# A graph layer on one Trainium2 core: edge ranges found to the edge, 17 gathers per 128 nodes, a ring of four

## The chip, the cores and the metric

One of the eight cores of a Trainium2 chip runs the kernel. The metric is the device time of one launch in microseconds (us). The engines are TensorE (PE, with its weight loads as PEld), VectorE (DVE), ScalarE (ACT), GpSimd (POOL) and SyncE (SP). They run their own instruction streams and wait for each other through semaphores.

## The reference

One layer over 12500 nodes with 256 channels and 200000 edges, sorted by destination. Everything is float32.

```python
xn = layernorm(x)
# relational graph convolution, 8 relations: mean over (relation, destination)
msg = xn[src] * edge_weight[:, None]
seg = edge_type * N + dst
h = segment_sum(msg, seg) / maximum(segment_sum(1, seg), 1)
gnn = einsum('rnc,rco->no', h.reshape(R, N, C), weight) + xn @ root + bias
# linear attention, 8 heads of 32, over all nodes: q, k = elu(.) + 1
mix = (q @ (k^T v)) / (q . sum(k) + 1e-6) @ wo + bo
x = x + gnn + mix
# mixture of 6 experts with 3 layers of 256 x 256, the best two of a router's softmax
x = x + ffn(layernorm(x))
```

Because the relation's weight acts on a sum, the kernel computes y[node, relation] = xn[node] @ weight[relation] for all nodes first. An edge then adds coefficient x y[src, type] to its destination, where the coefficient is its weight over the number of edges of the same destination and type.

## The kernel before, in words

The program has two phases, a block each. A matmul in float32 precision is made of three fast ones: each operand is split into a high part (ACT, a rounding copy) and a low part (DVE, the difference).

**First phase** (lines 85 to 762). A loop over 98 steps `u` of 128 nodes. PE computes keys and values (line 696, `pproj`) and the eight relations' products (`yb`), ACT copies the latter to `yst` (line 314, two buffers), SP stores them to the table `y_tab` in memory (line 242). Every fourth step a super-tile of 512 nodes is loaded, normalised, turned and stored as `xt_tab`. The function `edges(u)`, which DVE (line 531) and PE (line 714) have each, hangs work on the edges on single steps: the edge arrays are loaded twice, as 391 rows of 512 edges (`rows_i`) and as 125 rows of 1600 edges (`lin_d`, `lin_t`, `lin_w`, line 215). From the first, PE's transposes (`turn_rows`, line 707) and DVE's copies (`by_tile`, line 408) make tables that stay in SBUF with one column for each tile of 128 edges: destination `dst_t`, row of `y_tab` `idx_t`, coefficient `coef_t`. From the smallest and largest destination of each tile, `tiles_of_nodes` (line 419) finds for each 128 nodes the first tile of edges (`lo_row`) and by how many tiles it exceeds 18 (`more_row`). From the second, scans in both directions count the edges of the same destination and type; the coefficient goes to memory at step 80 as `coef_tab` (line 231), comes back at step 82 as rows (`crow`, line 235), and is turned at steps 86 to 90.

**Second phase** (from line 764). 25 super-tiles of 4 x 128 nodes; the last has two times 128. For each 128 nodes the edges are gathered tile by tile, 18 tiles from `lo` on; edges of other nodes in them match no column of the one-hot tile. A super-tile n thus has 72 gathers, in 12 portions p of 6:

- POOL: `portion(n, p)` (line 1045) waits until portion p - 3 has been used, then issues six indirect DMAs (line 1025), each of which gathers 128 rows of 1 KB from `y_tab` into the ring `ring`, which has three slots. `indices(n)` (line 1039) copies the row numbers from `idx_t` to `ring_i`. After the last super-tile two portions of a 26th, empty one are gathered.
- ACT: `high(n, p)` (line 1080) waits for the rows and writes coefficient x row to `row_hi` (two buffers, line 1088).
- DVE: `one_hot(n, p)` (line 1220) compares destinations with 0 to 127 into `sel` (two buffers), `low_rows(n, p)` (line 1225) writes the difference to `row_lo`. `tables(n)` (line 1209) copies destinations and coefficients of a super-tile.
- PE: `aggregate(n, p)` (line 1502) does two matmuls a tile, `sel` times high and low rows, into `acc`, and counts `portion_used`, which frees the slot.
- `leftover` (in each of the four) would handle, one by one, tiles beyond the 18.

The loop `iteration(i, plan)` (25 times, on PE, ACT and DVE) finishes super-tile i (layer norm, router, six experts) and in between aggregates super-tile i + 1 and computes its queries and attention. The order is written out by hand: portions 0 and 1 after the turned features, 2 after the first hidden layer, 3, 4, 5, 7, 9, 11 in front of the third layer of experts 0 to 5 (`AHEAD_W3`) and 6, 8, 10 behind that of experts 2, 3, 4 (`BESIDE_W3`). ACT does portions 6, 8 and 10 in halves between hidden features (line 1102 high part, 1104 full value), and, at the end of iteration i, portions 0 and 1 of super-tile i + 2, ahead of the root of the variance (line 1107) of the next iteration. PE's experts are line 1453, root sums and queries too.

**Between the phases**: SP loads the weights (`stage`, two buffers), ACT and DVE split three expert weights (lines 1158 and 1416) before they take any portion of super-tile 0; then all 12 portions of it follow without experts. `portions_before(n, p)` (line 944) turns a portion into a count.

## Time and profile before

| what | value |
|---|---|
| median of three runs | 3529.99 us (3527.38 to 3536.67) |
| the profiled execution | 3521.7 us, span 3519.7 us |
| mean granted clock of TensorE | 0.94 |
| first phase, from the start to the last store's wait | 0 to about 815 us |
| stage between the phases, to the first root of variance | 815 to 964 us |
| 24 loop iterations | 964 to 3477 us |
| last iteration | 3477 to 3520 us |

The page names a group of instructions by line, engine, operation and tiles (output <- inputs). PE, DVE, ACT and POOL are busy while they compute; POOL's `DMA_INDIRECT` is the time it takes to write a gather's descriptors. "Idle before" is the time the engine stood still ahead of an instruction, with what ended it; "issue" means that the profile shows nothing that it waited for.

### The profile page before, as it was taken

The page shows a single profiled execution, that of the slowest core. Times are in us where ns is not written, and L with a number is a line of the kernel's source. Part 1 is how long each engine was busy: PE and PEld are TensorE (multiplying, and loading weights), DVE is VectorE, ACT ScalarE, POOL GpSimd, SP SyncE. Part 2 cuts the span into 40 slices and gives each one's busy share as a digit, 9 for nine tenths or more (in the row PEclk, how much of TensorE's full clock was granted, in tenths as well). Part 3 has the DMA queues.
Part 4 walks back from the last instruction along what each step waited for, and adds up shares of the span by engine and source line. Part 5 has one row for each costly group of instructions (what it writes and reads, how often), then busy time and mean ns, then how long its engine had stood idle before and what let it go on. Part 6 is the DMA issues. An engine that isn't in the chain of part 4 may idle for free.

```text
span 3519.7 us, 49971 instructions
## 1 busy us (share of the span) xinstructions
PE 3073.8 (87%) x17125; PEld 2680.3 (76%) x17126; DVE 2454.4 (70%) x5692; ACT 2104.1 (60%) x4161; POOL 1975.6 (56%) x1932
## 2 busy tenths in 40 slices
PE   5999999994488988889988888888888898888887
PEld 4888888884377877878877777777787787777776
DVE  3458745323477777877777777778787777787775
ACT  4555555553366666666666666666666666666665
POOL 0000000003777777777777777777777777777773
PEclk9999999996599999999999999999999999999999
DMA  5445455545333333333343333333333333333331
GB/s 198 171 170 194 189 193 199 203 172 177 94 110 113 113 115 108 112 100 116 114 117 109 113 101 116 113 116 116 111 114 101 113 113 115 109 117 98 112 98 53
DMA packets 159285, 450.16 MB, mean 128 GB/s; under 512 B 33711, under 2 KB 79953, under 8 KB 140122
## 3 DMA queue, kind: packets, MB, share of 16 engines
q0 software_dynamic: 86976, 237.62, 23.9%
q1 hardware_dynamic: 68220, 205.82, 15.7%
q10 hardware_dynamic: 3826, 3.43, 0.3%
q8 instruction: 138, 2.26, 0.3%
q14 instruction: 125, 1.02, 0.1%
HBM read 303.73 MB, written 143.01 MB: 127 GB/s over the span
## 4 chain that ended last, share of the span: by engine, by line
POOL 35%; PE 19%; issue 17%; DVE 2%; ACT 2%; POOLq 1%; DVEq 0%; DMA 0%; ACTq 0%
POOL ring L1025 35%; PE bank L1453 13%; PE acc L1508 4%; DVE row_lo L1229 2%; ACT row_hi L1088 2%; PE bank L1598 1%; POOLq L1041 1%; PE bank L1480 1%; PE bank L1580 0%; DVE h_lo L1327 0%; POOLq L1042 0%; POOLq L951 0%; ACT ht L1104 0%; PE acc L1525 0%; PE acc L1453 0%
## 5 line engine op out<-in xcount | busy, mean ns | idle before, releaser
L1025 POOL DMA_INDIRECT ring<-y_tab,ring_i x1812 | 1945.3, 1074 | 682.7 <-issue 530.6
L1088 ACT ACTIVATE row_hi<-ring,coef_w 128x256 fp32r<-128x256 f32 x1812 | 764.0, 501 | 457.4 <-issue 397.4
L1229 DVE SCALAR_TENSOR_TENSOR row_lo<-ring,coef_w,row_hi 128x256 fp32r<-128x256 f32 x1806 | 740.5, 477 | 160.3 <-ACT row_hi L1088 160.3
L1508 PE MATMUL acc<-row_hi,sel 128*128 128x256 f32 x1800 | 521.6, 319 | 323.1 <-DVE row_lo L1229 323.1
L1102 ACT ACTIVATE h_hi<-bank,bias_t 128x512 fp32r<-128x512 f32 (+1 forms) x600 | 405.8, 676 | 445.6 <-PE bank L1453 433.8
L1508 PEld LDWEIGHTS acc<-row_hi,sel 128*128 128x128 f32 x1800 | 388.7, 216 | 357.1 <-DVE row_lo L1229 352.3
L1327 DVE TENSOR_TENSOR h_lo<-ht,h_hi 128x512 fp32r<-128x512 f32 (+1 forms) x600 | 401.8, 679 | 338.9 <-ACT ht L1104 336.7
L696 PE MATMUL yb<-wr_hi,xhl 128*128 128x512 f32 x1568 | 509.1, 395 | 0.0
L1508 PE MATMUL acc<-row_lo,sel 128*128 128x256 f32 x1800 | 505.3, 310 | 0.0
L1042 POOL COPY ring_i<-idx_t 128x18 int32 x104 | 26.2, 289 | 812.0 <-POOLq L88 810.6
L1104 ACT ACTIVATE ht<-bank,bias_t 128x512 f32<-128x512 f32 (+1 forms) x600 | 405.9, 676 | 27.9 <-DVE h_lo L1327 25.7
L314 ACT ACTIVATE yst<-yb 128x512 f32<-128x512 f32 x392 | 230.8, 595 | 320.0 <-PE yb L696 314.0
L1508 PEld LDWEIGHTS acc<-row_lo,sel 128*128 128x128 f32 x1800 | 393.0, 218 | 4.8
L1453 PE MATMUL bank<-ew_hi,h_hi 128*128 128x256 f32 x1176 | 351.7, 299 | 19.5 <-DVE h_lo L1327 18.8
L696 PEld LDWEIGHTS yb<-wr_hi,xhl 128*128 128x128 f32 x1568 | 294.6, 188 | 72.3
L1453 PE MATMUL bank<-ew_lo,h_hi 128*128 128x256 f32 x1176 | 339.7, 289 | 0.0
L1453 PE MATMUL bank<-ew_hi,h_lo 128*128 128x256 f32 x1176 | 338.7, 288 | 0.0
L696 PE MATMUL yb<-wr_lo,xhl 128*128 128x512 f32 x784 | 310.1, 396 | 0.0
L1222 DVE TENSOR_TENSOR sel<-iota_w,rel_w 128x768 fp32r<-128x768 f32 x301 | 286.2, 951 | 6.3 <-issue 6.3
L659 DVE TENSOR_TENSOR zk<-pproj,bkv_sb 128x256 f32<-128x256 f32 x98 | 41.6, 424 | 347.1 <-PE pproj L696 346.1
L1453 PE MATMUL bank<-h_hi,ew_hi 128*128 128x512 f32 (+1 forms) x600 | 260.4, 434 | 3.0 <-DVE h_lo L1327 3.0
L1453 PEld LDWEIGHTS bank<-ew_hi,h_hi 128*128 128x128 f32 x1176 | 232.1, 197 | 30.3 <-DVE h_lo L1327 28.1
(240 smaller groups left out, 5647.2 us busy)
## 6 DMA issues: line engine op xcount, KB each, us to landing
y_tab<-yst SPq DMA_DIRECT2D x97, 1024.0 KB, 3.8
ring<-y_tab,ring_i POOLq DMA_INDIRECT x1812, 2.8
xt_tab<-xhl SPq DMA_DIRECT2D x25, 1024.0 KB, 3.8
xc<-xt_tab SPq DMA_DIRECT2D x25, 1024.0 KB, 4.9
xs<-in_x SPq DMA_DIRECT2D x24, 512.0 KB, 5.9
x<-in_x SPq DMA_DIRECT2D x48, 256.0 KB
out<-y SPq DMA_DIRECT2D x24, 512.0 KB
stage<-in_L_ffn_expert_w SPq DMA_DIRECT2D x6, 768.0 KB, 11.5
```

Of the source, the lines that this page charges most:

```text
L314: act.activation(yst[:, h, 2 * b:2 * b + 2, :], yb[(YB * u + b) % 3][:, :].rearrange("p (r n) -> p r n", r=2), ACT.Copy).then_inc(y_ev, 1)
L659: dve.tensor_tensor(zk[:, h, :], pproj[:, 0:C], bkv_sb[:, 0:C], ALU.add)
L696: last = pe.matmul(out_ap, a, b, start=(i == 0), stop=(i == len(parts) - 1))
L1025: pool.indirect_dma_start(out=out_ap, out_offset=None, in_=y_tab[:, :], in_offset=bass.IndirectOffsetOnAxis(ap=idx_ap, axis=0)).then_inc(s ...
L1088: last = act.activation(row_hi[:, p % 2, q, :], ring[:, p % SLOTS, q, :], ACT.Copy, scale=coef_w[:, n % 2, c:c + 1])
L1102: act.activation(dest[:, m, 0:W], b[:, 0:W], ACT.Relu, bias=bias)
L1104: gone(act.activation(ht[:, m, 0:W], b[:, 0:W], ACT.Relu, bias=bias))
L1222: dve.tensor_tensor(sel[:, p % 2, :, :], iota_w[:, :].unsqueeze(1).to_broadcast([P, PT, NT]), rel_w[:, n % 2, p * PT:(p + 1) * PT].unsquee ...
L1229: last = dve.scalar_tensor_tensor(out=row_lo[:, p % SLOTS, q, :], in0=ring[:, p % SLOTS, q, :], scalar=coef_w[:, n % 2, c:c + 1], in1=row_ ...
L1327: dve.tensor_tensor(lo_[:, m, 0:W], ht[:, m, 0:W], hi[:, m, 0:W].bitcast(F32), ALU.subtract).then_inc(h_lo_set, 1)
L1453: last = pe.matmul(out_ap, a, b, start=(begin and i == 0), stop=(not more and i == len(parts) - 1), skip_group_check=more)
L1508: last = pe.matmul(into, sel[:, p % 2, q, :], half, start=False, stop=False, skip_group_check=True)
```

## The change

Each range of edges starts at its first edge instead of the first tile, so 17 tiles (2176 edges) take the place of 18. The first phase writes one table `etab` to memory, a row of three words for each edge (row of `y_tab`, destination, coefficient) with padding behind it, and SP loads of it 17 x 128 edges for each 128 nodes, 17 edges to a partition. Portions have 6, 6 and 5 tiles, and the ring has four slots, `row_hi` and `sel` three. The two portions of a 26th super-tile are left out. The splits of the three expert weights stand behind portions 2, 5 and 8 of super-tile 0. In the first phase the loads and transposes of rows of 512 edges go, except the destinations'; the first and last edge of a range are found with two gathers of destinations (`dpad`) and some twenty small DVE instructions.

```diff
-RANGE = 18
-PT = 6
-PARTS = SUB * RANGE // PT
-SLOTS = 3
+RANGE = 17
+SIZES = (6, 6, 5)
+PT = max(SIZES)
+PARTS = SUB * len(SIZES)
+SLOTS, BUFS = 4, 3
+PAD = (RANGE + 1) * P
+WEIGHTS_AT = (2, 5, 8)
...
# first phase, SP
-                for i, a in enumerate((dst, etype, src)):
-                    sp.dma_start(rows_i[:, i, 0:3, :], by_block(a)).then_inc(rows_in_e, 16)
...
+                sp.dma_start(rows_i[:, 0, 0:3, :], by_block(dst)).then_inc(rows_in_e, 16)
...
-                for a, into in ((dst, lin_d), (etype, lin_t), (ew, lin_w)):
+                for a, into in ((dst, lin_d), (etype, lin_t), (ew, lin_w), (src, lin_s)):
                     sp.dma_start(into[0:ROWS, :], by_row(a)).then_inc(lin_in, 16)
+                whole_tiles = E // P
+                sp.dma_start(dpad[0:whole_tiles, :].rearrange("(a t) k -> a (t k)", a=2),
+                             dst[0:whole_tiles * P].rearrange("(a k) -> a k", a=2)).then_inc(dpad_out, 16)
...
+                sp.wait_ge(pad3_set, 2)
+                sp.dma_start(etab[E:E + PAD, :].rearrange("(p k) c -> p (k c)", p=P),
+                             pad3[:, :, :].rearrange("p k c -> p (k c)")).then_inc(etab_out, 16)
...
                     if u == 80:
                         sp.wait_ge(coef_set, 1)
-                        sp.dma_start(by_row(coef_tab), lin_w[0:ROWS, :]).then_inc(coef_out, 16)
-                    if u == 82:
...
+                        sp.dma_start(etab[0:E, :].rearrange("(p k) c -> p (k c)", k=LIN),
+                                     lin3[0:ROWS, :, :].rearrange("p k c -> p (k c)")).then_inc(etab_out, 16)
...
# first phase, POOL
+                for i in range(2):
+                    pool.indirect_dma_start(out=two_i[:, i, :], out_offset=None, in_=dpad[:, :],
+                                            in_offset=bass.IndirectOffsetOnAxis(ap=tile_i[:, i:i + 1], axis=0)
+                                            ).then_inc(two_in, 16)
...
# first phase, DVE
+                    if u == 27:
+                        edges_of_nodes()
...
-                    if 87 <= u < 91:
-                        by_tile(u - 87 + M_COEF, coef_t, u - 87)
...
# second phase, SP
+                def load_table(n):
+                    if n >= 2:
+                        sp.wait_ge(portion_used, portions_before(n - 1, 0))
+                    for t in range(SUB):
+                        start = sp.value_load(lo_row[0:1, SUB * n + t:SUB * n + t + 1], min_val=0, max_val=E + P)
+                        sp.dma_start(tab[:, n % 2, t, :, :].rearrange("p k c -> p (k c)"),
+                                     etab[bass.ds(start, RANGE * P), :].rearrange("(p k) c -> p (k c)", k=RANGE)
+                                     ).then_inc(tab_in[n % 2], 16)
+
                 sp.sem_inc(y_stored, 16)
+                load_table(0)
+                load_table(1)
...
                 for s in range(SUPER - 2):
+                    load_table(s + 2)
                     sp.wait_ge(items_full, full(s, LOOP, "ft", 0))
...
# second phase, POOL
                 def portion(n, p):
+                    if p == 0:
+                        pool.wait_ge(tab_in[n % 2], 16 * SUB * (n // 2 + 1))
                     pool.wait_ge(portion_used, portions_before(n, p) - SLOTS + 1)
-                    for q in range(PT):
-                        c = p * PT + q
-                        rows(ring[:, p % SLOTS, q, :], ring_i[:, n % 2, c:c + 1], rows_in[p % SLOTS])
+                    for q, (t, k) in enumerate(tiles_of_portion(p)):
+                        rows(ring[:, p % SLOTS, q, :], tab_i[:, n % 2, t, k, 0:1], rows_in[p % SLOTS])
...
-                        if p == SLOTS:
-                            indices(n + 1)
...
-                for p in range(2):
-                    portion(SUPER, p)
...
# second phase, ACT
                     if more:
-                        for p in range(2):
-                            high(i + 2, p)
+                        if i + 2 < SUPER:
+                            for p in range(2):
+                                high(i + 2, p)
...
                 for p in range(PARTS):
                     high(0, p)
+                    if p in WEIGHTS_AT:
+                        j = WEIGHTS_AT.index(p)
+                        act.wait_ge(w_in[j], 16 * (KC + (j == 0)))
+                        if j == 0:
+                            act.activation(rw1_hi[:, :, :], stage_r, ACT.Copy)
+                        act.activation(w_hi[j][:, :, :, :], stage[j % 2][:, :, :, :], ACT.Copy).then_inc(w_hi_set, 1)
...
# second phase, DVE
                     for t in range(SUB):
-                        lo = dve.value_load(lo_row[0:1, SUB * n + t:SUB * n + t + 1], min_val=0, max_val=TILES - RANGE)
-                        cols = slice(t * RANGE, (t + 1) * RANGE)
-                        dve.tensor_scalar(rel_w[:, n % 2, cols], dst_t[:, bass.ds(lo, RANGE)], float(n * NS + t * NT), None,
+                        dve.tensor_scalar(rel_w[:, n % 2, t, :], tab[:, n % 2, t, :, 1], float(n * NS + t * NT), None,
                                           ALU.subtract)
-                        last = dve.tensor_copy(coef_w[:, n % 2, cols], coef_t[:, bass.ds(lo, RANGE)])
```

## Rows read from the trace of the kernel before

**Rows 1.** The page: busy time of the engines, and slices of the span.
```profile
PE 3073.8 (87%) x17125; PEld 2680.3 (76%) x17126; DVE 2454.4 (70%) x5692; ACT 2104.1 (60%) x4161; POOL 1975.6 (56%) x1932
...
POOL 0000000003777777777777777777777777777773
PEclk9999999996599999999999999999999999999999
```

**Rows 2.** The page: the chain that ended last, by engine.
```profile
POOL 35%; PE 19%; issue 17%; DVE 2%; ACT 2%; POOLq 1%; DVEq 0%; DMA 0%; ACTq 0%
```

**Rows 3.** The page: costliest groups; busy us, mean ns of one, idle before.
```profile
L1025 POOL DMA_INDIRECT ring<-y_tab,ring_i x1812 | 1945.3, 1074 | 682.7 <-issue 530.6
L1088 ACT ACTIVATE row_hi<-ring,coef_w 128x256 fp32r<-128x256 f32 x1812 | 764.0, 501 | 457.4 <-issue 397.4
L1229 DVE SCALAR_TENSOR_TENSOR row_lo<-ring,coef_w,row_hi 128x256 fp32r<-128x256 f32 x1806 | 740.5, 477 | 160.3 <-ACT row_hi L1088 160.3
L1508 PE MATMUL acc<-row_hi,sel 128*128 128x256 f32 x1800 | 521.6, 319 | 323.1 <-DVE row_lo L1229 323.1
```

**Rows 4.** The root of variance, all 25: duration ns, first and last start.
```profile
L1107 ACT ACTIVATE std_c<-mv_c,eps_ln x25: 295/297/299, 964.2 to 3477.0; 128x4 f32<-128x4 f32 x24, 128x2 f32<-128x2 f32 x1
```

**Rows 5.** Waits of POOL over the span: us in total, times, longest.
```profile
POOL ring L1025 <- issue: 530.6, 1753, 0.3
POOL ring L1025 <- PE acc L1508: 151.5, 58, 23.7
```

**Rows 6.** Timeline of POOL in one iteration: start, us, instruction, idle before.
```profile
1223.70 0.95 POOL L1025 DMA_INDIRECT ring<-y_tab,ring_i  x1 [2.35 <-PE acc L1508]
...
1283.75 1.49 POOL L1025 DMA_INDIRECT ring<-y_tab,ring_i  x1 [3.07 <-PE acc L1508]
1285.55 1.76 POOL L1025 DMA_INDIRECT ring<-y_tab,ring_i  x1 [0.30 <-issue]
```

**Rows 7.** Timeline of PE: first matmuls of portions 3, 6, 8, 10; one behind 6.
```profile
1194.65 0.39 PE L1508 MATMUL acc<-row_hi,sel 128*128 128x256 f32 x1 [2.31 <-DVE row_lo L1229]
...
1228.06 0.39 PE L1508 MATMUL acc<-row_hi,sel 128*128 128x256 f32 x1 [0.88 <-DVE row_lo L1229]
...
1229.59 0.39 PE L1453 MATMUL bank<-h_hi,ew_hi 128*128 128x512 f32 x1
...
1243.35 0.58 PE L1508 MATMUL acc<-row_hi,sel 128*128 128x256 f32 x1 [3.61 <-DVE row_lo L1229]
...
1260.19 0.58 PE L1508 MATMUL acc<-row_hi,sel 128*128 128x256 f32 x1 [3.58 <-DVE row_lo L1229]
```

**Rows 8.** Timeline of ACT and DVE, portions 3, 8 and 10.
```profile
1189.59 2.51 ACT L1088 ACTIVATE row_hi<-ring,coef_w 128x256 fp32r<-128x256 f32 x6 [3.87 <-issue]
...
1233.37 1.31 ACT L1088 ACTIVATE row_hi<-ring,coef_w 128x256 fp32r<-128x256 f32 x3 [0.91 <-issue]
...
1240.84 2.46 DVE L1229 SCALAR_TENSOR_TENSOR row_lo<-ring,coef_w,row_hi 128x256 fp32r<-128x256 f32 x6
...
1250.21 1.31 ACT L1088 ACTIVATE row_hi<-ring,coef_w 128x256 fp32r<-128x256 f32 x3 [1.16 <-issue]
```

**Rows 9.** Stretches: length, busy us of each engine, granted clock, DMA share, GB/s.
```profile
1195.00:1198.00 3.00, 3.00 (x17) 3.00 (x16) 2.56 (x19) 2.14 (x5) 2.27 (x3) 0.52 0.36 97
...
1244.00:1247.00 3.00, 3.00 (x15) 2.87 (x15) 3.00 (x7) 0.27 (x1) 2.13 (x3) 0.62 0.45 112
```

**Rows 10.** Timeline between the phases.
```profile
818.51 1.12 POOL L1025 DMA_INDIRECT ring<-y_tab,ring_i  x1 [0.66 <-POOL ring_i L1042]
...
839.17 0.60 ACT L1153 ACTIVATE kw_sb<-acc 128x512 f32<-128x512 f32 x1 [8.05 <-PE acc L1619]
...
866.14 1.67 POOL L1025 DMA_INDIRECT ring<-y_tab,ring_i  x1 [23.67 <-PE acc L1508]
```

**Rows 11.** First phase: eight transposes of PE, and DVE's waits for PE.
```profile
693.35 1.04 PE L689 MATMUL tb<-ident,xn 128*128 128x128 f32 x8
...
DVE zk L659 <- PE pproj L696: 346.1, 91, 7.7
```

**Rows 12.** Stretches at the start of the first phase, columns as in rows 9.
```profile
6.00:12.00 6.00, 0.00 (x0) 0.00 (x0) 1.48 (x8) 0.00 (x0) 0.00 (x0) 1.00 1.06 377
...
20.00:26.00 6.00, 0.00 (x0) 0.00 (x0) 0.00 (x0) 0.00 (x0) 0.00 (x0) 1.00 0.33 128
26.00:32.00 6.00, 0.00 (x0) 0.00 (x0) 0.00 (x0) 0.30 (x1) 0.00 (x0) 1.00 0.32 130
```

**Rows 13.** DMA issues: KB each, median us to landing.
```profile
xs<-in_x SPq DMA_DIRECT2D x24, 512.0 KB, 5.9
...
coef_tab<-lin_w SPq DMA_DIRECT2D x1, 781.2 KB
```

291 lines of the change are left out of this document (153 added, 138 removed).

## The prediction

> **What bounds the kernel now.** The shares come first. TensorE is busy for 87% of the span, GpSimd (POOL) for 56% of the whole but for almost all of the second phase; the granted clock is full in the first phase and a little under it in the second [rows 1]. The chain that ended last lies on POOL's gathers for 35%, on PE for 19%, and 17% is "issue", which beside the gathers is the fixed pause of 0.30 us before each one [rows 2]. So the second phase is paced by the gathers together with what PE does in the same iteration. The groups give their price: 1812 gathers take 1945.3 us, and their pauses 530.6 us, so one costs 1.366 us; an ACT scaling of a gathered tile is 0.50 us, the DVE difference 0.48 us, and every tile has two matmuls [rows 3]. An iteration holds 72 gathers, 98.4 us. The root of variance opens each of the 25 iterations, first at 964.2 and last at 3477.0 us: 24 loop iterations of 104.7 us each [rows 4]. The rest of POOL's iteration is about 1.2 us of index copies and about 5 us of waiting for a free slot of the ring: 151.5 us in 58 waits over the run, 23.7 of them one wait at the start of the phase [rows 5].
>
> I then looked at one iteration, PE from 1176.1 to 1281.8 us. POOL stands still twice, 2.35 us until portion 5 is used and 3.07 us until portion 0 of the next super-tile is [rows 6]. PE stands still at four of its twelve portions: 2.31 us at portion 3, 0.88 at 6, 3.61 at 8, 3.58 at 10 [rows 7]. These four have different causes, and that decides the forecast. At portion 3, ACT was idle 3.87 us because the rows had not landed, after POOL's late start: the ring caused it. At 8 and 10, ACT waited for rows only 0.91 and 1.16 us [rows 8]; the rest is the order of the work on ACT and DVE. ACT takes turns between hidden features and halves of a portion, and only after the last of these may DVE make its one-hot and its six differences, which end at 1243.3 us, as PE starts [rows 7, 8]. A longer ring doesn't move that part.
>
> **The change, part by part.**
>
> *68 gathers instead of 72.* POOL's iteration falls to 68 x 1.366 = 92.9 us, and the index copies leave POOL. PE has eight matmuls fewer; twelve of them take from 1228.06 to 1229.59 [rows 7], 0.13 us each, so 1.0 us. Portion 8 now has five tiles and lies on the ACT and DVE path of the last paragraph: 0.42 us on ACT, 0.41 + 0.16 us on DVE, 1.0 us. The longest of the 98 ranges of destinations that the inputs draw has 2166 edges, 17 tiles hold 2176, so the leftover loop stays empty, as it was.
>
> *Ring of four.* Portion 8 then waits for portion 4 and portion 3 for portion 11 of the super-tile before; both are long used, so POOL's two waits go. That gives PE the 2.31 us at portion 3 and ACT's 0.91 and 1.16 us at 8 and 10. After the stall at portion 3 the granted clock was 0.52 for 3 us [rows 9], the lower of the two levels (1.2 GHz against 2.4), which costs 1.5 us; I count it as gone with the stall. The stalls at 8 and 10 shrink to 1.7 and 2.4 us; the first was followed by such a stretch too (0.62), the short one of 0.88 us by none. I take half of its 1.4 us, 0.7. Bounds for these clock terms: nothing, and all three stretches gone, some 4.5 us.
>
> Sum for an iteration: 1.0 + 1.0 + 2.31 + 2.07 + 1.5 + 0.7 = 8.6 us, so 96.1 us, which stands above POOL's 92.9. What is late next is DVE's part of portions 8 and 10, then POOL. 24 x 8.6 = 206 us less. The third buffer of high rows and one-hot tiles is worth nothing here: at portions 6, 8 and 10 the slot had been used an iteration step earlier. The DVE copies of coefficients (four of about 0.17 us each) also go, while DVE is ahead; nothing.
>
> *Tables through SP.* Four register loads and DMAs, 26 KB each, at the top of an iteration, for the super-tile after next. Their wait for the last use of the old table is met by then; behind it on SP stand the loads of the turned features and of x and the store, all with tens of us of slack. POOL wants the table when about 75 us have passed. Cost nothing; without that cover, the 5.9 us that a load of SP's takes to land [rows 13]. In front of the phase it is on the path: the first gather ran at 818.5 us from a copy; now it waits for four loads and their landing, +3.5 us (bounds 2 and 8). The eight loads also stand ahead of the loads of wq and root, which come 7 us later; ACT is free for portion 0 after its copy at 839.2 us, 21 us after the first gather, and the portion needs 6.5 us on ACT, DVE and PE; with 7 us more and a start 3.5 us later that makes 31 us, and POOL asks for the slot 33 us after its start [rows 10]. Just covered; what it lacks would be a wait of a few us.
>
> *Weights between portions.* The wait of 23.67 us [rows 10] is POOL with all three slots full, while ACT and DVE split three weights before they take portion 0. Now they take three portions first, and a split (2.8 us of ACT, 3.4 us of DVE) fits between portions that come every 8 us. 23.7 us less, with 5.5 us for four gathers and 1.2 us for copies: with the +3.5, this stage gets 26.9 us shorter.
>
> *The end.* Two portions of a 26th super-tile, which nobody used, go. ACT stood behind them before the last root of variance; its own input was ready 1 us earlier. -1 us.
>
> *First phase.* PE is without a gap there. 48 transposes of edge rows go, at eight in 1.04 us [rows 11]: -6 us, of which I take 5. DVE's new edge search (some 20 small instructions at step 27) and the strided writes at steps 5 and 6 are under 5 us each, in steps of 7.4 us of which DVE waits 3.8 us for PE in the mean [rows 11]: nothing. Two DMAs are not hidden so well. A load of 125 rows ran with 0.33 of the DMA engines and 128 GB/s, where 0.32 is five of sixteen [rows 12]. The table is stored from 125 rows as well, 2344 KB instead of 781 KB [rows 13]: 18.3 us instead of 6.1, and the y_tab store behind it on SP's queue lands some 6 us after the third step wants its buffer. +6 us (bounds 0 and 12). At the very start 1.6 MB of well spread loads go, but a fourth load of 125 rows and a copy of 781 KB from memory to memory in two rows come. At the rates of rows 12 it takes between 2.1 us (all engines, 377 GB/s) and 31 us (one engine, 26 GB/s); x and y_tab wait behind it on the same queue. I take +8 us, nearer the low end because most of it overlaps the wait for weights (bounds -3 and +25). The Trainium skill ("DMA: Bandwidth & Descriptors", "Why a DMA increments its semaphore by 16 and not by 1") says that a DMA uses the largest number of engines up to 16 that divides the slowest dimension of both sides. The trace agrees for 125 rows, five. By that rule the copy in two rows would use two engines; an estimate from it is 15 us of copy where my sum has 8 us of delay, so 3312 us instead of 3305.
>
> **The sum.** Against the profiled execution's 3521.7 us (span 3519.7): +9 for the first phase, -26.9, -206, -1, together -225: 3297 us. The median of the runs, 3530.0, lies 8.3 us above the profiled one; with that, 3305 us.
>
> **Rivals.**
> *A. POOL stays the bound.* If the short stalls and all three low-clock stretches go, PE's iteration falls under POOL's. DVE's part of a gather's slowness stays: gathers take 0.95 us when undisturbed, and the 0.12 us more in the mean comes 72 times an iteration; if it belongs to the portions and not to the gathers, an iteration is 68 x 1.25 + 8.9 = 93.9 us. 24 x 10.8 = 259: 3252 us. For it: PE is at full clock wherever it doesn't wait. Against: rows 7 and 8, the order on ACT and DVE. 20%.
> *B. The stalls keep their place.* ACT and DVE, not the rows, hold back portions 8 and 10, the clock falls as often, and portion 3 gains only its 2.31 us: 4.3 us an iteration, 103 us: 3408 us. 12%.
> *C. Slower: gathers from a table with stride.* The index of a gather now lies every 12 bytes in a table row instead of every 4. If reading it made a gather longer, it would decide from 104.7 / 68 = 1.54 us each, against 1.37 now. Nearest row: a gather that was disturbed took 1.76 us [rows 6]; at 1.76 + 0.30 an iteration is 140 us and the run, with the 80 gathers ahead of the first iteration, some 4400 us. The trace has nothing for it, since each gather reads one element of a partition either way. 3%.
> *D.* The ranges are not what the change says, leftovers run, or tables come late: 2%.
>
> **How the numbers follow.** My forecast has 63%. Its own range is 3265 to 3345 us, from the bounds of the clock terms (24 x 1.5) and of the first phase. To hold the time 8 times in 10 the range takes in A down to 3240 and B up to 3400. A difference under 0.3% (10 us) could not be told from none here. All of the forecast, A and B are faster: 95%. C and half of D give 4% slower, 1% stays within 0.3%.
>
> **What would show it.** 1700 gathers of about 1.07 us and no ring_i copies; no 23.7 us wait, and POOL's waits on PE either gone or moved to where it runs four portions ahead; PE waits on row_lo about 5 us an iteration instead of 10.5, at portions 8 and 10 and not at 3; the distance of the roots of variance 96 us; a step near the table's store in the first phase with a wait of ACT on y_tab. A distance of 94 us with POOL without a pause would be A; 100 us with 3.6 us stalls left would be B; a gather longer than 1.5 us would be C. A first phase more than 25 us longer would show the start mis-sized.

## The result, and the profile after the change

The changed kernel takes 3323.52 us (median; 3321.86 to 3328.22), the kernel before beside it 3528.68 us (3521.63 to 3536.67). The ratio is 0.942, 95% interval 0.940 to 0.944: 205 us less. The prediction was 3305 us in a range of 3240 to 3400. The profiled execution took 3322.96 us with a span of 3321.3 us, so it can be set against the prediction's own sum, which began at 3521.7 us.

The page of the changed kernel: busy time, two of the slices, the chain that ended last, and the groups that answer to [rows 1 to 3].

```profile
PE 2967.5 (89%) x16875; PEld 2584.7 (78%) x16876; DVE 2380.5 (72%) x5481; ACT 2045.9 (62%) x4049; POOL 1890.5 (57%) x1721
...
POOL 0000000000777777777777777777777777777771
PEclk9999999999579999999999999999999999999999
...
POOL 23%; PE 20%; DVE 11%; ACT 9%; issue 9%; DVEq 2%; DMA 1%; SPq 0%; POOLq 0%; ACTq 0%
...
L1085 POOL DMA_INDIRECT ring<-y_tab,tab x1700 | 1884.1, 1108 | 1121.7 <-DMA tab<-etab 583.1
L1137 ACT ACTIVATE row_hi<-ring,tab 128x256 fp32r<-128x256 f32 x1700 | 719.0, 510 | 114.5 <-issue 111.6
...
L1277 DVE SCALAR_TENSOR_TENSOR row_lo<-ring,tab,row_hi 128x256 fp32r<-128x256 f32 x1700 | 698.4, 479 | 66.7 <-ACT row_hi L1137 64.6
L1557 PE MATMUL acc<-row_hi,sel 128*128 128x256 f32 x1700 | 468.1, 308 | 214.7 <-DVE row_lo L1277 214.6
```

There are 1700 gathers, as forecast, but one takes 1108 ns in the mean, where it took 1074. PE's waits for the low parts fell from 323.1 to 214.7 us. ACT's "issue" idle, which in front of this line is time until the rows have landed, fell from 397.4 to 111.6 us. The chain, which was POOL and issue for 52%, is now POOL and issue for 32%, and PE, DVE and ACT for 40%.

The root of variance, all 25, which gives the length of an iteration as [rows 4] did:

```profile
L1156 ACT ACTIVATE std_c<-mv_c,eps_ln x25: 296/297/300, 961.9 to 3277.8; 128x4 f32<-128x4 f32 x24, 128x2 f32<-128x2 f32 x1
```

(3277.8 - 961.9) / 24 = 96.50 us, against 104.7 before and 96.1 predicted. The waits over the whole span, as in [rows 5]:

```profile
POOL ring L1085 <- DMA tab<-etab: 583.1, 1, 583.1
POOL ring L1085 <- issue: 506.7, 1661, 0.9
...
PE acc L1557 <- DVE row_lo L1277: 214.6, 85, 10.1
POOL ring L1085 <- PE acc L1557: 31.8, 38, 3.8
```

POOL waits 31.8 us for slots where it waited 151.5. The first line is not part of the phase: POOL has nothing to do until the first table is there. In steady running POOL has hardly any time left. One stretch of it, columns as in [rows 9], and POOL's pauses in it:

```profile
1100.00:3100.00 2000.00, 1820.47 (x11043) 1616.60 (x11041) 1635.42 (x3860) 1330.72 (x2671) 1556.55 (x1412) 0.96 0.40 116
...
POOL ring L1085 <- issue: 420.8, 1379, 0.9
```

Of these 2000 us POOL is busy 1556.55 and stands 420.8 in pauses between gathers; that makes 1977. PE is busy 1820.

PE in one iteration, the waits for the low parts that answer to [rows 7]:

```profile
1175.36 0.39 PE L1557 MATMUL acc<-row_hi,sel 128*128 128x256 f32 x1 [1.14 <-DVE row_lo L1277]
...
1207.86 0.39 PE L1557 MATMUL acc<-row_hi,sel 128*128 128x256 f32 x1 [1.31 <-DVE row_lo L1277]
1221.19 0.38 PE L1557 MATMUL acc<-row_hi,sel 128*128 128x256 f32 x1 [1.96 <-DVE row_lo L1277]
1236.62 0.58 PE L1557 MATMUL acc<-row_hi,sel 128*128 128x256 f32 x1 [2.77 <-DVE row_lo L1277]
```

They are the first matmuls of portions 3, 6, 8 and 10, as before. The four stalls are 7.2 us together; before they were 10.4. Behind the last two the clock still falls:

```profile
1236.60:1239.60 3.00, 2.98 (x13) 2.98 (x14) 2.94 (x7) 0.00 (x0) 2.39 (x3) 0.50 0.40 104
1221.00:1224.00 3.00, 2.81 (x14) 2.52 (x15) 2.91 (x7) 0.00 (x0) 2.12 (x3) 0.70 0.35 107
1207.80:1210.80 3.00, 2.94 (x19) 2.68 (x20) 2.91 (x8) 0.00 (x0) 2.39 (x3) 1.00 0.35 98
```

At 0.50 the clock is the lower of its levels, 1.2 GHz; at 0.70 it is there for part of the stretch; behind the stall of 1.31 us it is the full 2.4 GHz.

Between the phases, the timeline of POOL, PE and DVE, against [rows 10]:

```profile
831.67 0.95 POOL L1085 DMA_INDIRECT ring<-y_tab,tab  x1 [583.14 <-DMA tab<-etab]
...
842.44 1.19 PE L1503 MATMUL bank<-xc,wqr_hi 128*128 128x512 f32 x2 [21.72 <-DMA xc<-xt_tab]
...
865.54 2.20 POOL L1085 DMA_INDIRECT ring<-y_tab,tab  x1 [3.37 <-PE acc L1557]
868.05 6.14 POOL L1085 DMA_INDIRECT ring<-y_tab,tab  x1 [0.30 <-issue]
869.15 3.37 DVE L1468 TENSOR_TENSOR ew_lo<-stage,ew_hi 128x3072 fp32r<-128x3072 f32 x1
872.41 0.96 DVE L1271 TENSOR_TENSOR sel<-iota_w,rel_w 128x768 fp32r<-128x768 f32 x1
874.50 2.94 POOL L1085 DMA_INDIRECT ring<-y_tab,tab  x1 [0.31 <-issue]
...
894.44 3.36 DVE L1468 TENSOR_TENSOR ew_lo<-stage,ew_hi 128x3072 fp32r<-128x3072 f32 x1 [0.58 <-ACT ew_hi L1211]
894.65 3.97 POOL L1085 DMA_INDIRECT ring<-y_tab,tab  x1 [0.31 <-issue]
...
920.25 3.36 DVE L1468 TENSOR_TENSOR ew_lo<-stage,ew_hi 128x3072 fp32r<-128x3072 f32 x1 [0.58 <-ACT ew_hi L1211]
920.85 3.57 POOL L1085 DMA_INDIRECT ring<-y_tab,tab  x1 [0.30 <-issue]
```

The wait of 23.67 us has shrunk to 3.37. But a gather that runs while DVE makes the low part of an expert weight takes 6.14, 3.97 or 3.57 us instead of 0.95. The ends say more: the gather of 3.97 us ends at 898.62, 0.82 us after the subtraction beside it, the one of 3.57 us 0.81 us after its subtraction, and the one of 6.14 us ends at 874.19, 0.82 us after the one-hot (872.41 to 873.37) that DVE made right behind the subtraction. The gathers of 2.20 and 2.94 us run beside row differences and one-hots, not beside a subtraction of weights. Before the change the same three subtractions (843.10 to 849.72 and 856.28 to 859.64) ran while POOL stood in its long wait.

### The profile page after: what moved, and what is told of

It reads as the page before. It is cut to its first block, busy times and chain, and to the rows that moved or that the text cites. A ratio compares the mean times of both kernels' runs of the same rounds, so it can differ in the third digit from the quotient of the medians.

```text
span 3321.3 us, 48604 instructions
## 1 busy us (share of the span) xinstructions
PE 2967.5 (89%) x16875; PEld 2584.7 (78%) x16876; DVE 2380.5 (72%) x5481; ACT 2045.9 (62%) x4049; POOL 1890.5 (57%) x1721
## 3 DMA queue, kind: packets, MB, share of 16 engines
q8 instruction: 136, 2.23, 0.3%
## 4 chain that ended last, share of the span: by engine, by line
POOL 23%; PE 20%; DVE 11%; ACT 9%; issue 9%; DVEq 2%; DMA 1%; SPq 0%; POOLq 0%; ACTq 0%
POOL ring L1085 23%; PE bank L1503 14%; DVE row_lo L1277 5%; PE acc L1557 4%; ACT row_hi L1137 4%; ACT ht L1153 3%; ACT h_hi L1151 2%; DVE h_lo L1374 1%; DVEq L1431 1%; PE bank L1648 1%; PE bank L1530 1%; DMA ring<-y_tab,tab 1%; DVE xn_c L1394 1%; DVE x L1379 1%; DVE qf L1241 1%
## 5 line engine op out<-in xcount | busy, mean ns | idle before, releaser
L1085 POOL DMA_INDIRECT ring<-y_tab,tab x1700 | 1884.1, 1108 | 1121.7 <-DMA tab<-etab 583.1
L1137 ACT ACTIVATE row_hi<-ring,tab 128x256 fp32r<-128x256 f32 x1700 | 719.0, 510 | 114.5 <-issue 111.6
L1277 DVE SCALAR_TENSOR_TENSOR row_lo<-ring,tab,row_hi 128x256 fp32r<-128x256 f32 x1700 | 698.4, 479 | 66.7 <-ACT row_hi L1137 64.6
L1557 PE MATMUL acc<-row_hi,sel 128*128 128x256 f32 x1700 | 468.1, 308 | 214.7 <-DVE row_lo L1277 214.6
L1557 PEld LDWEIGHTS acc<-row_hi,sel 128*128 128x128 f32 x1700 | 348.6, 205 | 243.2 <-DVE row_lo L1277 238.0
L1557 PE MATMUL acc<-row_lo,sel 128*128 128x256 f32 x1700 | 453.6, 298 | 0.0
L1557 PEld LDWEIGHTS acc<-row_lo,sel 128*128 128x128 f32 x1700 | 351.4, 207 | 5.3
L1271 DVE TENSOR_TENSOR sel<-iota_w,rel_w 128x768 fp32r<-128x768 f32 (+1 forms) x300 | 271.9, 906 | 5.7 <-issue 5.6
L1503 PE MATMUL bank<-h_lo,ew_hi 128*128 128x512 f32 (+1 forms) x600 | 251.5, 419 | 0.0
L1503 PE MATMUL bank<-h_hi,ew_lo 128*128 128x512 f32 (+1 forms) x600 | 248.3, 414 | 0.0
```

Source lines behind the costliest of these rows:

```text
L1085: pool.indirect_dma_start(out=out_ap, out_offset=None, in_=y_tab[:, :], in_offset=bass.IndirectOffsetOnAxis(ap=idx_ap, axis=0)).then_inc(s ...
L1137: last = act.activation(row_hi[:, p % BUFS, q, :], ring[:, p % SLOTS, q, :], ACT.Copy, scale=tab[:, n % 2, t, k, 2:3])
L1271: dve.tensor_tensor(sel[:, p % BUFS, 0:size, :], iota_w[:, :].unsqueeze(1).to_broadcast([P, size, NT]), rel_w[:, n % 2, t, k:k + size].uns ...
L1277: last = dve.scalar_tensor_tensor(out=row_lo[:, p % SLOTS, q, :], in0=ring[:, p % SLOTS, q, :], scalar=tab[:, n % 2, t, k, 2:3], in1=row_h ...
L1503: last = pe.matmul(out_ap, a, b, start=(begin and i == 0), stop=(not more and i == len(parts) - 1), skip_group_check=more)
L1557: last = pe.matmul(sums(t), sel[:, p % BUFS, q, :], half, start=False, stop=False, skip_group_check=True)
```

## The experiments

Two theories were weighed for the iteration. By the first, POOL's gathers pace it. By the second, the order in which ACT and DVE take their work does. Four more questions concern the stage between the phases and the first phase. All kernels are the changed one with the edit shown. The chip of the first four runs had the kernel before at 3517.13 us, which at the ratio of 0.942 puts the changed kernel at about 3313 us there. The two chips of the other runs ran every kernel more slowly (the kernel before took 3926.03 and 3992.88 us, the clock granted to the changed kernel was 0.90 instead of 0.955), so their runs are compared only with their neighbours.

### The ring and the third buffer taken back

```diff
-SLOTS, BUFS = 4, 3
+SLOTS, BUFS = 3, 2
```

> The kernel after the change with three ring slots and two buffers of high rows and one-hot tiles, as before it, all else kept (17 gathers, tables, weights between portions). Changed kernel: 3323 us, 96.5 us an iteration. Theory P (POOL now paces the loop: 68 gathers of 1.108 + 0.30 us are 95.7 of the 96.5 us) and theory O (the order of work on ACT and DVE paces it, as I forecast) agree that the ring matters: POOL waits about 5 us an iteration again and PE 2.3 us at portion 3: 100 to 102 us an iteration, 3410 to 3460 us. Rival R (the ring was worth nothing, the fewer gathers are the whole gain): 3323 us within 15.

3468.78 us (3465.25 to 3476.24), ratio 0.987 (0.984 to 0.990). The root of variance, and waits between 1100 and 3100 us:

```profile
L1156 ACT ACTIVATE std_c<-mv_c,eps_ln x25: 296/298/301, 972.1 to 3432.7; 128x4 f32<-128x4 f32 x24, 128x2 f32<-128x2 f32 x1
```

```profile
ACT row_hi L1137 <- issue: 221.4, 99, 6.2
POOL ring L1085 <- PE acc L1557: 189.9, 63, 6.7
PE acc L1557 <- DVE row_lo L1277: 177.8, 78, 3.8
```

An iteration is 102.5 us, 6.0 more than with the ring of four: some 145 us of the 205. Both theories had named 100 to 102 us and 3410 to 3460 us, and it came out a little above that. POOL's wait for slots in this stretch is 189.9 us against 23.0 in the changed kernel. The edit takes back the third buffer too, but ACT waits for a free buffer only 3.9 us in the whole run, so nearly all of it is the ring. Against the 104.7 us of before, all the rest of the change is worth 2.2 us an iteration with the short ring: POOL gives the time of the four gathers back in front of full slots (before, it waited 100.2 us in this stretch).

### Eighteen gathers per 128 nodes, ring of four

```diff
-RANGE = 17
-SIZES = (6, 6, 5)
+RANGE = 18
+SIZES = (6, 6, 6)
```

> The kernel after the change with 18 tiles a range (portions of 6, 6, 6) and the ring of four kept. Theory P: four gathers more cost 4 x 1.41 = 5.6 us an iteration, 24 x 5.6 + 6 = 141 us: 3464 us. Theory O: POOL has room, so only eight matmuls and the sixth tile of portion 8 count, 2.0 us an iteration, 48 us, and 6 us ahead of the loop: 3377 us. 3420 us lies between the two.

3408.14 us (3385.42 to 3410.58), ratio 0.968 (0.963 to 0.973).

```profile
L1156 ACT ACTIVATE std_c<-mv_c,eps_ln x25: 295/298/299, 971.8 to 3367.7; 128x4 f32<-128x4 f32 x24, 128x2 f32<-128x2 f32 x1
```

```profile
POOL ring L1085 <- issue: 435.2, 1428, 0.3
...
POOL ring L1085 <- PE acc L1557: 4.6, 15, 0.3
```

99.8 us an iteration, and in 2000 us POOL waits 4.6 for slots: here POOL does pace. The theory of the order had forecast 3377 us and that of the gathers 3464, and the time is between them. The gathers' own mean of 1.089 us (1960.2 us in 1800 gathers) and the pause of 0.30 give 72 x 1.39 = 100.0 us. So the shorter range is worth 3.3 us an iteration once the ring is longer, where the prediction had 2.0. The two parts seem to help each other: everything but the shorter range gives 4.9 us (104.7 - 99.8), everything but the ring 2.2, and the whole change 8.2. The sum of the first two is 7.1, though it counts the rest of the change twice (the tables, no index copies, which no run has by themselves). The difference of 1.1 us or more is small for kernels on two chips that are 0.3% apart.

### Sixty-four gathers per iteration

```diff
+                        if n and q == 0 and p % 3 == 2:
+                            continue
                         rows(ring[:, p % SLOTS, q, :], tab_i[:, n % 2, t, k, 0:1], rows_in[p % SLOTS])
```

(and the counts of rows to wait for; ACT and DVE read the rows of the next tile in place of those left out)

> From the second super-tile on, POOL leaves out the first gather of each portion of five (64 gathers instead of 68 an iteration); ACT and DVE read the second tile's rows twice instead, so that ACT, DVE and PE do the same work as before. This leaves 4 of 68 tiles of edges out of the sums. Theory P: 5.6 us less an iteration until ACT, DVE or PE bounds it, 60 to 135 us less: 3190 to 3265 us. Theory O: no change, 3310 to 3330 us.

Left out are the gathers of four of the 68 tiles of edges of an iteration; the rest of the work on those tiles stays, on the wrong rows. 3319.95 us (3319.32 to 3322.61), ratio 0.945 (0.942 to 0.948): nothing gained, where the theory of the gathers had 3190 to 3265 us and that of the order 3310 to 3330. The iteration is 96.1 us. POOL now has time, and spends it in front of a full ring:

```profile
POOL ring L1085 <- PE acc L1559: 150.2, 75, 6.1
PE acc L1559 <- DVE row_lo L1279: 137.3, 63, 2.9
```

PE's waits are as in the changed kernel (140.6 us in the same stretch). At 68 gathers POOL is nearly full, but it does not set the time; at 72 it does.

### VectorE prepares the next rows ahead of an expert's low part

```diff
                         if e == 0:
                             best_two(i, plan)
+                        if more and e in BESIDE_W3:
+                            prepare(i + 1, BESIDE_W3[e])
                         low("h1", e + 1)
-                        if more and e in BESIDE_W3:
-                            prepare(i + 1, BESIDE_W3[e])
```

> DVE prepares portions 6, 8 and 10 before the low parts of the next expert's first hidden layer instead of behind them; the same instructions, POOL untouched. Theory P: POOL's 95.7 us stay, so at most 1 us an iteration: 3300 to 3330 us. Theory O: PE's stalls at portions 8 and 10, 1.7 and 2.4 us, and the clock stretches behind them go: 4 to 6 us an iteration, 3180 to 3230 us.

3332.7 us (3322.99 to 3339.48), ratio 0.948 (0.945 to 0.952): nothing gained, rather a little lost. The theory of the order had 3180 to 3230 us and is refuted as the sole cause; that of the gathers had 3300 to 3330. Waits in the same stretch:

```profile
ACT row_hi L1137 <- issue: 334.7, 117, 6.5
...
PE bank L1503 <- DVE h_lo L1374: 97.9, 43, 6.2
...
PE bank L1549 <- DVE xn_c L1394: 47.2, 20, 3.2
PE acc L1557 <- DVE row_lo L1277: 23.3, 24, 2.5
```

The wait that the edit aims at is gone (140.6 to 23.3 us), and as much comes back elsewhere: PE now waits for the low part of the hidden features (97.9 us) and for the normalised rows, and ACT for rows to land (334.7 against 42.8 us). POOL is busy 1571.1 us and pauses 424.1 of 2000: full. A gather is 1.116 us here in the mean, with its pause 1.42, and 68 of them are 96.6 us of the iteration's 96.7. So relief on one side alone does nothing. That looks like two limits of one length, about 96 us, and called for both at once.

### Both at once

> The edits of e3_fewer_gathers and e4_dve_order together (64 gathers an iteration, some tiles' rows read twice, so 4 of 68 tiles of edges are left out of the sums; DVE prepares portions 6, 8 and 10 earlier). Alone each gave nothing. Theory B (two bounds of nearly the same length: POOL's 68 x 1.41 = 95.7 us and the PE, ACT and DVE order's 96 us): together they gain, 3 to 5.6 us an iteration, 3190 to 3250 us. Rival S (a third thing sets the pace, such as PE's own work or the path through the layer norm at the head of an iteration): 3310 to 3335 us, as each alone.

The two edits above together; four of 68 tiles of edges are left out here too. On the first of the slower chips: 3668.11 us (3666.05 to 3679.17), ratio 0.935 (0.928 to 0.941). How much the unchanged kernel gains on this chip is not known, so this says little; the next two runs stand side by side on the other slow chip.

> The changed kernel with nothing altered, as the yardstick of this chip for the three runs beside it. By the first comparison its ratio to the kernel before is 0.942 (0.940 to 0.944); both theories expect that. On the chip of the last four runs everything was slower and it is not known what this ratio was there.

3817.52 us (3811.38 to 3836.86), ratio 0.957 (0.953 to 0.960). The change gains less here than on the chip of the first comparison.

> Both of the two suspected bounds of the iteration eased at once: 64 gathers instead of 68 per iteration (four of 68 tiles of edges are left out of the sum) and VectorE splits the gathered rows of the next iteration ahead of the expert that it now does first. Each alone moved the time by nothing (ratios 0.945 and 0.948). Theory of two equal bounds (POOL's gathers, and TensorE waiting for the low parts): together they give 3 us or more in each of the 24 iterations, ratio 0.905 to 0.925. Theory of a third bound (the chain of TensorE, ScalarE and VectorE through the experts alone): at most 1 us per iteration, ratio 0.935 to 0.945.

3733.48 us (3712.41 to 3743.84), ratio 0.935 (0.932 to 0.939): 84 us under the unchanged kernel beside it, 3.5 us an iteration. By the size of the gain the theory of two equal limits has it (3 us or more); by the ratio the theory of a third limit has it (0.935 to 0.945, against 0.905 to 0.925). The profile says that this chip cannot decide. The stretch from 1100 to 3100 us of the unchanged kernel, then of this one:

```profile
1100.00:3100.00 2000.00, 1640.80 (x9173) 1441.76 (x9171) 1360.78 (x3214) 1100.73 (x2211) 1239.34 (x1163) 0.88 0.33 96
```

```profile
1100.00:3100.00 2000.00, 1672.44 (x9557) 1469.21 (x9556) 1413.56 (x3353) 1145.69 (x2305) 1220.76 (x1141) 0.91 0.33 95
```

Already in the unchanged kernel POOL is busy only 1239 us here and waits 347.6 us for slots, so the gathers do not set the time; the granted clock in this stretch is 0.88, where it was 0.96 on the first chip. Roots of variance 116.2 us apart became 111.6 us. PE's busy share times these lengths is 95.3 and 93.3 us an iteration. The matmuls are the same, 533 an iteration in both, and the granted clock is 0.91 instead of 0.88: 2.0 us of the 4.6 is shorter busy time of PE at the higher clock, and the rest is shorter waiting. Neither edit was run alone on this chip, and with POOL idle for so long the gain may be that of the order on DVE alone. Whether both edits together would gain on a chip where POOL is full stays open.

### The weights split ahead of the portions, as before the change

```diff
+                for j in range(3):
+                    act.wait_ge(w_in[j], 16 * (KC + (j == 0)))
...
                 for p in range(PARTS):
                     high(0, p)
-                    if p in WEIGHTS_AT:
-                        j = WEIGHTS_AT.index(p)
```

(and the same on DVE)

> The changed kernel with the three splits of expert weights in front of portion 0, as before the change. The changed kernel's first root of variance is at 961.9 us. Theory: POOL fills its four slots and waits some 15 to 20 us for portion 0; the gathers that DVE's splits stretch to 6.1, 4.0 and 3.6 us now fall into that wait, which gives back 8: the first root of variance 8 to 15 us later. Rival: the order is worth nothing because the stretched gathers and the late portion 0 eat it: within 3 us.

3810.84 us (3801.17 to 3820.51), ratio 0.970 (0.961 to 0.979). PE's first matmul of portion 0:

```profile
897.13 0.58 PE L1555 MATMUL acc<-row_hi,sel 128*128 128x256 f32 x1 [17.79 <-DVE row_lo L1276]
```

In its three neighbours with the new order the first root of variance comes at 974.3, 981.6 and 982.6 us, here at 1003.6: 21 to 29 us later, more than the 8 to 15 expected. Here portion 0 begins at 897.13 us, in the neighbour with six splits at 879.24. POOL waits 33.60 us for the slot, where the expectation had 15 to 20. POOL stands still while the splits run, so no gather is stretched by them, but gathers of 2.54 and 2.94 us (905.03) beside row differences and one-hots are there:

```profile
900.34 1.54 POOL L1085 DMA_INDIRECT ring<-y_tab,tab  x1 [33.60 <-PE acc L1555]
902.18 2.54 POOL L1085 DMA_INDIRECT ring<-y_tab,tab  x1 [0.30 <-issue]
```

In the whole time the order is not told apart: the intervals of these runs of two executions overlap.

### Each split in six instructions

```diff
-                        dve.tensor_tensor(w_lo[j][:, :, :, :], stage[j % 2][:, :, :, :], w_hi[j][:, :, :, :].bitcast(F32),
-                                          ALU.subtract).then_inc(w_split_c, 1)
+                        for e in range(EXPERTS):
+                            last = dve.tensor_tensor(w_lo[j][:, e, :, :], stage[j % 2][:, e, :, :],
+                                                     w_hi[j][:, e, :, :].bitcast(F32), ALU.subtract)
+                        last.then_inc(w_split_c, 1)
```

> DVE's three differences of expert weights (3072 columns, 3.36 us each) are issued as six of 512 columns. Rival (the gather is slowed by the amount of DVE's traffic, not by the length of the instruction): gathers stay at 3 us and more in sum over the split.

3773.47 us (3764.0 to 3782.93), ratio 0.960 (0.951 to 0.970). The first stretched gathers stay, beside six short instructions in a row:

```profile
884.29 6.49 POOL L1085 DMA_INDIRECT ring<-y_tab,tab  x1 [0.30 <-issue]
891.09 2.93 POOL L1085 DMA_INDIRECT ring<-y_tab,tab  x1 [0.30 <-issue]
```

Those of 3.97 and 3.57 us are gone; no later gather up to 945 us took over 1.8. So the stretching is tied to these subtractions, and cutting them removes it in two places of three; in the third the gather ends at 890.78, 0.82 us after the one-hot that stands behind the six. It outlasts the end of one instruction, against the first theory, and the other two gathers are short, against the second. The first root of variance is at 974.3 us, 8 us earlier than in the neighbour below, but that is not shown to come from the cut: POOL waited 15.79 us for portion 0 here and 8.97 there, the 80th gather ended at 968.38 and 966.18 us, and two runs below with the same program up to that point have their first root 9.6 us apart.

### The second table after the tokens

```diff
                 load_table(0)
-                load_table(1)
...
                 load_w(0, e_w1, 0)
+                load_table(1)
```

> SP loads the second super-tile's table behind the loads of wq, root, the turned features and the first weights instead of ahead of them. Theory: four register loads and DMAs of about 1.07 us each no longer stand ahead, so PE starts 4.3 us earlier (842.4 to 838.2 us), POOL's wait of 3.4 us for portion 0 goes, and the first root of variance is 3 us earlier. Rival (POOL sets the end of this stage from its first gather on, whatever PE does): the same to 1 us beyond the 3.4.

3789.41 us (3785.34 to 3793.48), ratio 0.965 (0.955 to 0.974).

```profile
844.97 1.20 PE L1503 MATMUL bank<-xc,wqr_hi 128*128 128x512 f32 x2 [18.71 <-DMA xc<-xt_tab]
```

In the three neighbours PE's first matmul of the stage is at 848.12, 848.73 and 849.72 us, so the four loads did delay it by 3 to 5 us. The first root of variance (982.6 us) is no earlier than in the neighbours (974.3 and 981.6 with the new order), and the whole time shows nothing that could be told apart.

### Four mends, and the order on top

```diff
-                    if u == 80:
-                        sp.wait_ge(coef_set, 1)
+                    if 77 <= u < 81:
+                        part = slice((u - 77) * PART, (u - 76) * PART)
+                        sp.wait_ge(coef_set, u - 76)
...
-                             dst[0:whole_tiles * P].rearrange("(a k) -> a k", a=2)).then_inc(dpad_out, 16)
+                             dst[0:whole_tiles * P].rearrange("(a k) -> a k", a=22)).then_inc(dpad_out, 16)
```

(beside the splits in six and the later table). The second run has these four and makes the one-hots of portions 6, 8 and 10 earlier:

```diff
+                        if more and e in BESIDE_W3:
+                            one_hot(i + 1, BESIDE_W3[e])
                         low("h1", e + 1)
...
                         if more and e in BESIDE_W3:
-                            prepare(i + 1, BESIDE_W3[e])
+                            low_rows(i + 1, BESIDE_W3[e])
```

> Four small things put right that the prediction missed or undersized: the table of coefficients stored in four parts between units instead of in one (TensorE stood 9.6 us for it), the copy of the padding rows in 22 rows instead of 2 (part of 4.0 us at the start), the second range's table loaded after the tokens of the first (TensorE's start in the stage between the phases 3 to 4 us earlier), and VectorE's split of each expert weight in six instructions (stretched gathers, 8 us on the slower chip). Theory that each stands on the critical path: 9 + 2 + 3 + 4 to 8, together 18 to 22 us under the unchanged kernel beside it, ratio to it 0.993 to 0.9945. Theory that POOL's gathers set everything from the first gather on: only the 9.6 and the start count, 10 to 12 us, ratio 0.9965.

3781.37 us (3766.24 to 3796.76), ratio 0.947 (0.943 to 0.951), against 0.957 (0.953 to 0.960) of the unchanged kernel beside it: 36 us less, 0.9905 of its time, more than either theory had (18 to 22 and 10 to 12 us). PE's first matmul of the stage:

```profile
830.87 1.19 PE L1505 MATMUL bank<-xc,wqr_hi 128*128 128x512 f32 x2 [17.13 <-DMA xc<-xt_tab]
```

It was at 849.94 us. The first gather comes at 824.64 instead of 836.34, and PE's 9.6 us behind the store of the table are gone. The first root of variance is 24.4 us earlier (968.9 against 993.3). The profiled executions are 40.2 us apart, and the other 16 us are 0.7 us an iteration (115.5 against 116.2), for which none of the edits has a reason. The copy in 22 rows instead of two did nothing: it landed after 12.6 instead of 12.8 us, and PE's first wait is 45.5 instead of 45.2. Of that landing SP's record of the issue itself is 8.73 and 8.82 us.

> The four mends of the run beside it, and VectorE builds the one-hot tiles of the next iteration ahead of the expert it now does first, and the low parts of the rows behind it as now. If the wait of TensorE for the low parts is what this moves, 0 to 2 us per iteration, down to 40 us under the run beside it; if the gathers bound the iteration, the same as the run beside it within 6 us.

3800.1 us (3782.3 to 3816.48), ratio 0.952 (0.948 to 0.956). Neither of the two expectations: not less, and 19 us above its neighbour, though the two intervals overlap. An iteration is 116.5 us. The first root of variance is at 959.3 us, 9.6 us earlier than in the run beside it, though the program up to there is the same: so much can such a single reading vary here. Neither way of changing the order on DVE gained anything, all of the preparation on the first chip and the one-hots alone on this one.

## Why the prediction was right, point by point

**The iteration** was to lose 8.6 us and lost 8.2; 24 times that is 197 us where the sum had 206. Its parts hold less exactly, and that they add up so well is partly luck. The ring is worth 6.0 us by the first run, against 2.31 + 2.07 + 1.5 + 0.7 = 6.6, and the shorter range 3.3 by the second, against 2.0. In the iteration shown the stall at portion 3 is still there, 1.14 us instead of 2.31, because ACT waited 2.66 us for its rows; in the ones that begin near 2119 and 2698 us it is gone, but portion 6 waits 2.23 and 2.14. At 8 and 10 PE waits 1.96 and 2.77 us where 1.7 and 2.4 were forecast. From 1100 to 3100 us PE's waits for the low parts fell from 198.0 to 140.6 us, which is 10.4 and 6.8 an iteration: 3.6 less, where 2.31 + 2.07 = 4.4 were forecast, and 6.8 left instead of 5. PE's busy share times the length of an iteration fell from 92.37 to 87.84 us (granted clock 0.94 and 0.96). Eight matmuls are 1.0 of these 4.5 us and the clock terms had 2.2, so some 1.3 us came from where the forecast had put none; that made up for the waits. The clock still falls behind portion 8, though less (0.70), and behind 10 (0.50). That the stalls at 8 and 10 belong to the order on DVE was right: with that order changed, PE's waits for the low parts fell to 23.3 us.

**The term that was mis-sized** is POOL's 68 x 1.366 = 92.9 us. It took the mean of a gather as fixed. The mean rose from 1.074 to 1.108 us, so POOL needs 68 x 1.408 = 95.7 us, within a microsecond of the iteration. Rival A, with gathers at 1.25 us and its 93.9 us, is refuted by the same row: above 0.95 us the gathers of an iteration took 72 x 0.124 = 8.9 us before and take 68 x 0.158 = 10.7 now. Why they take more is not shown; a shorter iteration has nearly the same DVE work in less time. Of the margin of 3.2 us of POOL under PE's iteration that the prediction saw, 0.8 is left.

**Which of the two sets the time** is settled in part. POOL alone doesn't: with 64 gathers nothing is gained. PE's wait for the low parts alone doesn't: without it nothing is gained either, and POOL is full. That both share the bound fits, but the runs that should show it fell on chips with another bound, so this stays open.

**Between the phases** the forecast was -26.9 us and the profile gives -12.6: the first root of variance moved from 964.2 to 961.9, with 10.3 us more in the first phase. This is the term that failed; the range held it. The start of the gathers was right (13.2 us later, of which 10.3 from the first phase and 2.9 for the four loads, forecast 3.5). The wait went from 23.67 to 3.37 us, and these 3.4 us are the first part of the 14.3 by which the stage fell short, since the sum had taken off all of the 23.7. What was left out are the gathers beside the splits: (6.14 + 3.97 + 3.57) - 3 x 0.95 = 10.8 us. Together these are 14.2 us. Over all gathers the count agrees: above 0.95 us the first 84 of before took 11.1 us and the first 80 of now take 21.5, 10.4 more. The gathers of 2.20 and 2.94 us have their like in the run with the splits ahead, so the new places of the splits did not make them. A second omission was smaller in its effect. The eight table loads hold SP:

```profile
826.26 8.48 SPq L1036 DMA_DIRECT2D tab<-etab  x8
```

The prediction followed them to wq and root and not to the tokens behind these. PE began the stage at 842.44 instead of 824.08 us, 18.4 us later, 10.3 of them from the first phase. That shows as POOL's 3.37 us in front of the full ring, "a wait of a few us", as the prediction had it in words and not in its sum. The stretching was in no row of before, because POOL stood still when the splits ran. The prediction costed the moved instructions on ACT and DVE and not what they do to POOL, whose cover, the wait, it took away at the same time.

**The first phase** was forecast at +9 and came to +10.3: kv_bd, which DVE makes at its end, starts at 820.76 instead of 810.48 us. The start was to cost 8 us and cost 4.0 (PE's first wait 39.5 against 35.6). The store of the table was to cost 6 and cost more: ACT waits 13.09 us for y_tab at 700.05, and PE 9.6 behind it.

```profile
700.05 0.60 ACT L332 ACTIVATE yst<-yb 128x512 f32<-128x512 f32 x1 [13.09 <-DMA y_tab<-yst]
700.70 0.79 PE L752 MATMUL yb<-wr_hi,xhl 128*128 128x512 f32 x1 [9.58 <-ACT yst L332]
...
700.00:706.00 6.00, 5.30 (x19) 4.72 (x20) 0.00 (x0) 2.78 (x6) 0.00 (x0) 0.50 0.21 87
```

Behind the wait the granted clock was 0.50, the lower level, for 6 us; from 700 to 706 us of the kernel before it was full. In the run with the store in four parts the 9.6 us are gone and kv_bd starts 11.7 us earlier (813.77 against 825.49), so the store cost some 12 us, wait and clock together. With the 4.0 us at the start that leaves about -5.4 of the 10.3 for the transposes, of which -5 was taken. The bounds (-3 to 25, and 0 to 12) held both.

The fourth load of 125 rows looks like the others of [rows 12]; a stretch of the changed kernel while the last of these loads run:

```profile
26.00:32.00 6.00, 0.00 (x0) 0.00 (x0) 0.00 (x0) 0.00 (x0) 0.00 (x0) 1.00 0.32 129
```

The copy in two rows landed after 13.1 us for 781 KB. The Trainium skill ("DMA: Bandwidth & Descriptors", "Why a DMA increments its semaphore by 16 and not by 1") gives the number of engines as the largest number up to 16 that divides the slowest dimension of both sides, and the estimate from it was 15 us. By that rule 22 rows would have had eleven engines instead of two, yet the landing went from 12.8 to 12.6 us. Either the rule doesn't hold for this copy, or something else held it: the loads around it keep the queues busy in that time, and most of the landing is SP's issue (8.82 and 8.73 us). No run tells the two apart.

**The end** was -1 and is +0.8 us (3321.3 - 3277.8 = 43.5 against 42.7).

The sum: +10.3 - 12.6 - 197 + 0.8 = -198.5 us, from 3519.7 to 3321.3. The profiled execution is 26 us above the 3297 of the prediction: 14 us are the stage between the phases, 9 us the iterations and 3 us the first phase and the end. The median lies only 18.5 us above its 3305, because the forecast had added 8.3 us from the profiled execution to the median and the runs show 0.6: that is luck.

## What to carry to other kernels

When a wait is taken away, look at what ran beside the waiting engine: it never met that work, and the trace of before has no row for the meeting. Two parts that relieve one loop (a longer ring, fewer gathers) may not add: with the rest of the change they gave 4.9 and 2.2 us an iteration, together 8.2. When an engine is nearly full, take its price per instruction with a margin: 34 ns on each of 68 gathers took 2.3 of the 3.2 us by which POOL was to stand under PE.

## What was not expected of the hardware

An indirect gather of POOL and a VectorE instruction with two inputs in SBUF don't run beside each other freely. Alone a gather is busy 0.94 or 0.95 us; beside a subtraction of 128 x 3072 (3.36 us) it took 3.17 to 6.55 us in every run that had them between the portions, on three chips, and in the loop, beside one-hot tiles, row differences and the like, 1.41 and 1.47 us (1204.84 and 1195.14) and once 3.92 (1157.56). Of the 53 gathers over 1.15 us between 1100 and 1400 us, 40 end 0.79 to 0.85 us after the end of a DVE instruction, of the 161 shorter ones 23. That looks like a gather which waits for a gap in DVE's work and then needs 0.82 us; no experiment tested it. The Trainium skill ("SBUF — State Buffer", "Who interferes with whom") says that such a subtraction contends with GpSimd's reads only, and infers that descriptors are written all the same. Here the gathers were held up; whether by reading their indices or by writing descriptors no run tells, and the measured times decide that they are held up.

Behind a store of 2344 KB from 125 partitions, issued on SP's queue, ACT waited 13.09 us for a y_tab store of the same queue. With the table stored in four parts, one per step, ACT's longest such wait was 3.7 us (3.8 before the change) and PE had none.
